# The channel-average products of a fused convolution and attention kernel move into the middle of a convolution step

## What is computed

```
x = x + sign_conv3x3(groupnorm(x))                 # depthwise, signs of x and of the kernel
x = x + relu(batchnorm(ma + sa))                   # of v = groupnorm(x):
    gate = sigmoid(fc(mean(v)) + fc(max(v)))       # one per channel and image
    xc   = v * gate
    m    = mean of xc over the channels            # one value per pixel
    ma   = xc * sigmoid(state-space scan along m)
    sa   = xc * sigmoid(conv7x7(m, max of xc over the channels))
```

## Time and profile before

| | |
|---|---|
| median of 3 runs | 3325.71 us (3324.7 to 3326.61) |
| span of the profiled execution | 3373.7 us |
| time of the profiled execution beside its span | not given by the page |
| PE, DVE, ACT busy in the span | 77%, 88%, 80% |
| L1440, the convolutions, x4032 | 855.4 us busy on PE |
| L900, the copies of the averages, x224 | about 0.35 us each on ACT |

### The profile page before, as it was taken

How to read it: one execution, slowest core, us unless ns; L and a number is a source line. 1 busy time by engine, 2 the same in 40 slices (tenths; PEclk the granted TensorE clock), 3 DMA queues, 4 the chain that set the end, 5 groups by cost and what they waited for, 6 DMA issues and landing times. The chain is left out here.

```text
span 3373.7 us, 50742 instructions
## 1 busy us (share of the span) xinstructions
PE 2587.4 (77%) x17105; PEld 1657.5 (49%) x17105; DVE 2976.3 (88%) x4060; ACT 2701.0 (80%) x3772; POOL 56.8 (2%) x111
## 2 busy tenths in 40 slices
PE   7899999999999999999976333333776776766676
PEld 5566666666566666665432000000555555555555
DVE  8788999889998889988886999998999899888787
ACT  6788888888888888887763888887888888877777
POOL 3000000000000000000001100000000000000000
PEclk9999999999999999999986555555877778777767
DMA  8899999999999999998755999996999999999997
GB/s 318 328 374 399 386 367 366 364 368 401 374 364 365 369 398 384 366 367 335 274 129 122 380 420 419 420 421 261 382 428 430 428 426 420 415 386 374 373 369 289
DMA packets 199056, 1227.97 MB, mean 364 GB/s; under 512 B 29792, under 2 KB 38936, under 8 KB 157644
## 3 DMA queue, kind: packets, MB, share of 16 engines
q1 hardware_dynamic: 195884, 1223.41, 91.1%
q0 software_dynamic: 2976, 2.00, 0.3%
HBM read 805.14 MB, written 420.17 MB: 363 GB/s over the span
## 5 line engine op out<-in xcount | busy, mean ns | idle before, releaser
L1440 PE MATMUL psum<-signs,taps 128*128 128x448 f16 x4032 | 855.4, 355 | 29.4 <-DVE signs L1071 14.4
L1554 PE MATMUL psum<-signs,picked 12*128 12x448 bf16 x896 | 334.4, 517 | 340.4 <-DMA signs<-gate_scratch 276.6
L1945 ACT ACTIVATE stage<-psum 128x512 f32<-128x512 f32 x784 | 407.5, 614 | 209.1 <-DMA out_dram<-stage 186.7
L1440 PEld LDWEIGHTS psum<-signs,taps 128*128 128x128 f16 x4032 | 386.8, 98 | 351.7 <-issue 33.8
L1965 DVE SCALAR_TENSOR_TENSOR xc<-xt,curs,psum 128x1792 f32<-128x1792 f32 x222 | 452.0, 2077 | 121.7 <-PE psum L1554 119.2
L835 ACT ACTIVATE xt<-psum 128x896 f32<-128x896 f32 x416 | 378.0, 910 | 151.8 <-PE psum L1338 128.0
L1757 DVE SCALAR_TENSOR_TENSOR xc<-xt,curs,psum 128x1792 f32<-128x1792 f32 x224 | 455.8, 2077 | 34.0 <-PE psum L1554 33.1
L1691 ACT ACTIVATE xc<-xc 128x1792 f32<-128x1792 f32 x224 | 380.0, 1697 | 95.9 <-DVE xc L1757 95.9
L1122 DVE CUSTOM_DVE_ANT_0 xt<-scratch,xt 128x896 f32<-128x896 int8 x416 | 435.7, 1084 | 14.2 <-ACT scratch L843 14.2
L1338 PE MATMUL psum<-ident,stage 128*128 128x128 f32 x3066 | 410.2, 276 | 16.4 <-DMA stage<-x_dram 10.6
L1933 ACT ACTIVATE xc<-xc,bn,curs 128x1792 f32<-128x1792 f32 x224 | 411.1, 1899 | 7.6 <-DVE xc L1965 4.2
(11 more groups left out here) (222 smaller groups left out, 2830.4 us busy)
## 6 DMA issues: line engine op xcount, KB each, us to landing
xt<-x_scratch SPq DMA_DIRECT2D x210, 1792.0 KB
out_dram<-stage SPq DMA_DIRECT2D x112, 1792.0 KB, 13.6
stage<-x_dram SPq DMA_DIRECT2D x219, 896.0 KB, 9.0
xc<-x_scratch SPq DMA_DIRECT2D x210, 896.0 KB, 8.2
x_scratch<-xt SPq DMA_DIRECT2D x208, 896.0 KB, 8.5
x_scratch<-last_unit SPq DMA_DIRECT2D x16, 896.0 KB, 8.9
signs<-ssm_scratch SPq DMA_DIRECT2D x14, 448.0 KB, 4.6
xc<-ssm_scratch SPq DMA_DIRECT2D x14, 448.0 KB, 5.0
```

Of the source, the lines that this page charges most:

```text
L1440: return nc.tensor.matmul(turn[h % 2][:, b * 512:b * 512 + HB], taps[:, j, t, :], signs[:, j, r:r + RT // 2, dw:dw + W], start=t == 0, sto ...
L1554: last = nc.tensor.matmul(dst[:, b, :], picked[:, b * P:(b + 1) * P], gate_rows[:, s * BW:(s + 1) * BW], start=True, stop=True)
L1945: nc.scalar.activation(outs[n % 2][:, 2 * k:2 * k + 2, :].rearrange("p t c -> p (t c)"), out_ps[k % 4], ACT.Identity).then_inc(staged, 1)
```

## The change

`channel_sums` for strip h - 5 is issued in the middle of convolution h, after tap 5 and the turned tile (for h = 1 between the two halves of the convolution), where it stood behind the convolution. ScalarE's `average` moves from behind `pack` to in front of it. The waits stay the same ones. Not moved are step 13 of images that have a successor, strip 9, and everything after the 16 images.

```diff
@@ ScalarE, image(i), step h
                             max_rows(i - 2)
+                        at = strip_at(i, h, 5)
+                        if at and h >= 1 and not (last and more):
+                            average(*at)
                         pack(i, h, first)
                         if last and more:
                             evacuate(i + 1, NTILE - 2)
                             evacuate(i + 1, NTILE - 1)
                         if h == 1 and channels:
                             hidden(i - 1)
-                        if (at := strip_at(i, h, 5)) and h >= 1:
+                        if at and last and more:
                             average(*at)
@@ TensorE, image(i), step h
+                        at = strip_at(i, h, 5)
+
+                        def sums_between():
+                            if at and h >= 1 and not (h == last and more):
+                                pe.wait_ge(conv_packed, i * NP + h)
+                                channel_sums(*at)
+
...
                             pe.wait_ge(signs_made, i * NP + sign_at(1, j) + 1)
+                            sums_between()
                             for t in range(9):
...
+                                if t == 5:
+                                    sums_between()
                                 tap(0, t)
                                 ins = tap(1, t)
...
-                        at = strip_at(i, h, 5)
                         if h == last and more:
...
                             else:
-                                if h >= 1:
-                                    pe.wait_ge(conv_packed, i * NP + h)
-                                    channel_sums(*at)
                                 blocks_back(*at)
```

## The result

| | before | changed |
|---|---|---|
| median of 18 runs each | 3326.16 us | 3340.27 us |
| ratio, 95% interval | | 1.0035 (1.0026 to 1.0044) |
| the profiled execution: its own time, its span | span 3373.7 us | 3327.41 us, 3325.7 us |

The kernel became slower, and the forecast of 3323.5 us (3314 to 3333) missed it. The ratio leaves disturbed executions out, the medians don't; the ratio stands for 11.6 us.

What follows compares the result with a forecast made beforehand. VectorE paces an image's first part, TensorE the second, linked by the store's landing before convolution 6. Dense steps -3.2 and step 1 +1.0 gave -2.2 us from 3325.71: 3323.5 us, range 3314 to 3333.

Steps and rivals of the forecast that it cites:

- (4): Step 1: the average delays pack, `hidden` and L1362's products by 0.35 us; 1.0 us lost, between 0 and 4.9.
- A: Theory of the experiments: longer idle time at step 1 lets the granted clock fall, and slow taps make the image late.
- (3): TensorE's order in dense steps: 0.03 us less per step over 106 steps, 3.2 us gained, between 0 and 6.4.
- (1): Wait for the copy at convolutions 3 to 5: TensorE starts up to 0.89 us earlier, worth nothing behind VectorE and landing.
- the copy is the bound: Faster rival: profiled waits for L900 are on the path, so their 13.7 us go; 3312.0 us, chance 0.15.
- (2): Wait at convolution 6: L900 still waits for the same store landing, which hangs on VectorE; gain 0.
- L900 still has its 14 waits for the DMA: Sign for right: the averages' copy keeps its 14 waits for the store, total within 2 us.
- (5): Step 5: the pack waits with L900 for the landing; the tile's copy still fits by 0.17 us; counted 0.
- the sign that I had named for "wrong": At step 5: convolution 6 does not follow the end of L900 within 0.2 us.
- ScalarE's place in line: Slower rival: step 5's 0.17 us margin fails, delaying convolution 6 up to 0.89 us an image; 3336.0 us, chance 0.13.

Runs made afterwards that it cites:

- e3: Changed kernel with nine transposes of the identity, result unread, ahead of the gate's products at step 1; 3320.81 us, ratio 0.9972.
- e2: Kernel before with the change in step 1 alone; 3339.41 us, ratio 1.0027.
- f2: Changed kernel with four unread transposes of the identity ahead of the gate's products at step 1; 3329.71 us, ratio 1.0012.
- f3: Changed kernel with nine unread transposes of the identity behind the gate's products, ahead of convolution 2; 3352.82 us, ratio 1.0066.
- f4: Repeat run: changed kernel with nine unread transposes ahead of the gate's products at step 1; 3321.58 us, ratio 0.9986.
- e4: Changed kernel's order on TensorE, but ScalarE's old order with the average behind the pack; 3345.59 us, ratio 1.004.
- f1: Changed kernel with ScalarE's copy of the hidden layer ahead of average and pack at step 1, nothing added; 3321.25 us, ratio 0.9986.

## Why the prediction was wrong

**The step that failed is (4), Step 1.** It counted 3 x 0.35 = 1.0 us, between 0 and 4.9, for an average that delays the pack. Two things were left out. First, it noted "TensorE already waits there, 1.09 us" and did not ask what the sums had done there: they filled 0.89 us of the wait, and taking them out made it 1.98. The order of the instructions shows this at step 1; I had looked at the dense step and at step 5. Second, it priced the wait by what it delays and not by what follows it on TensorE. The two stretches of the earlier trace rows had a granted clock of 1.00, and I took that as given. The delay itself has the size that was counted: step 1 is 0.46 us longer in the mean of the thirteen images, and in e3, where it is 0.40 longer, nothing is lost by it. The term that was put at nothing is the clock in step 2, which lasts 8.40 us in the mean in place of 6.98. Altogether the first steps of thirteen images cost 11.03 us more, and that this is A is shown by e2, e3, f2 and f3.

The trace of before had a warning. In step 1 of image 6 TensorE waits 2.32 us for a tile's copy, and the clock falls once, behind that wait; it is back at 1.00 by convolution 2. Its timeline and its stretch, where the clock is again the third number from the right:

```profile
647.48 0.25 PE L1356 MATMUL psum<-fc_in,w 128*16 128x2 f32 x4 [2.32 <-ACT xt L835]
```
```profile
648.00:650.00 2.00, 2.00 (x19) 1.18 (x11) 2.00 (x5) 2.00 (x3) 0.00 (x0) 0.50 0.00 0
```

**(3), the dense step**, was right in mechanism and size. The forecast was 6.72 us plus an entry of 0 to 0.06 behind the sums, 0.03 less a step in the middle; measured 0.042 less, so the entry costs 0.01. Term by term the eight taps were set at 1.53 plus the entry and took 1.54, the maxima 0.76 and 0.76, the tile ahead of the sums 0.86 and 0.85. Over the 106 steps that is 4.5 us in place of 3.2. Where the clock holds it is nearly all that is left of the change: in e3 the parts from convolution 6 to the next image need 773.63 us in place of 777.49, those from convolution 0 to 6 565.63 in place of 566.46. The runs agree with it and are too coarse for the size: f4's interval stands for 1 to 8 us, and e3's takes in 1. By the rule of the Trainium skill that the prediction cites (TensorEngine Tiling (Array Packing), Key Properties: a change of the tiling mode drains TensorE), with the changes counted alone, the term would have been 0; the steps measured decide against that. In a dense step the weight load still sits idle at both changes, 0.17 and 0.36 us after in place of 0.37 and 0.36, so the changes are there, and their price differs with the neighbours; why, no run here shows.

**(1), the waits for the copy**, was worth nothing, as said, though nearly all of them went: 9.6 us, 27 times, became 1.4 us, 3 times. They should have been left at convolution 6 in every image; they were not, since TensorE came late to it. Where the clock holds (e3), the gain over before is that of the dense step and not the 13.7 us of *the copy is the bound*, so that rival fell.

**(2), the landing.** "L900 still has its 14 waits for the DMA" was wrong for the changed kernel. Line L900 in it, answering to the earlier trace rows:

```profile
  DMA feat_scratch<-hsum: 9.6, 8
  PE psum L1376: 6.3, 21
who waited for it (us, times):
  PE psum L1450: 4.0, 4
```

and in e3, where the first steps have their old pace, the 14 are back, though not "with the same total within 2 us" (13.8 before): the copy no longer has the pack ahead of it, so ScalarE comes to the wait earlier.

```profile
  DMA feat_scratch<-hsum: 23.7, 14
```

So the landing bounds convolution 6 only while TensorE is early; in the changed kernel TensorE's own list is later.

**(5), the pack behind the landing**, and the slower rival built on it: in the image shown, the copy of step 5 now waits 0.20 us for the landing, and convolution 6 follows 0.63 us behind its end, because TensorE is busy with its own list until then. In the timeline of ScalarE and of TensorE after, answering to the earlier trace rows:

```profile
1201.29 0.36 ACT L900 ACTIVATE hsum<-psum 128x224 f32<-128x224 f32 x1 [0.20 <-DMA feat_scratch<-hsum]
...
1202.28 2.07 PE L1450 MATMUL psum<-signs,taps 128*128 128x448 f16 x10
```

This was the sign that I had named for "wrong", and it pointed at TensorE. The sign was good; the range had no case in which TensorE itself is late at step 5. The count of 0 for (5) held where it was put to the test: in e3, with the landing in its old place, no turned tile of step 6 waits for a copy, and convolutions 6 and 7 are 6.72 or 6.73 us apart in every image. The time came out slower, as in the rival of ScalarE's place in line, but not by its mechanism: e4 takes that away and stays slow.

What stays open: the profiled execution of the changed kernel is 7 us above before in this phase, the ratio of all runs says 11.6. The other executions have no trace; that they have more falls was not shown. Part of the difference may lie behind this phase, where the ten traces other than those of before and e4 differ by 10.6 us (1749.1 in e3, 1759.7 in e2).

## What to carry to other kernels

When an instruction is moved, look at the wait that it leaves as closely as at the one that it shortens: work that stands inside a wait may be what keeps TensorE from idling long enough to lose its clock. Price a longer wait on TensorE also by the matmuls behind it at half speed, and ask whether TensorE sets the pace there: the eleven images with a fall took 10.5 us more than before, the four of f1 no more. If a wait can't be shortened, useless matmuls in it can be worth their place; the same matmuls behind it made this kernel slower still.

## What was not expected of the hardware

The wait ahead of the gate was 1.83 to 2.15 us in the changed kernel, and the granted clock fell in 11 images of 13, though not in two with 2.15. It fell in 7 behind 1.34 to 1.71 us (f2), in none behind 0.79 to 1.17 (e3, f4) or 1.09 (before); yet in f1 it fell in 4, behind 1.02 us, and in five others with the same 1.02 it did not. So the length of the last wait alone does not decide it. The places differ in what stands ahead of the wait: nine transposes in e3, the maxima directly behind the hidden layer in f1. What of this matters no run here tells.
